# Decoder layer on one core: self and cross sums copied out in two halves, weighs in plain order, and maxima four further ahead

## The reference, cut to what matters

```python
q, k, v = _heads(x @ Wq + bq), _heads(x @ Wk + bk), _heads(x @ Wv + bv)       # 16 heads of 16
att = jnp.einsum('bhqd,bhkd->bhqk', q, k) * scale                            # causal, 512 x 512
y = jnp.einsum('bhqk,bhkd->bhqd', jax.nn.softmax(att, axis=-1), v)
qc, kc, vc = ...                                                              # from x and from the context
attc = jnp.einsum('bhqd,bhkd->bhqk', qc, kc) * scale                         # 512 x 1024
y = y + jnp.einsum('bhqk,bhkd->bhqd', jax.nn.softmax(attc, axis=-1), vc)
return y @ Wp + bp
```

## Time and profile before

| | |
|---|---|
| median of 3 runs | 2287.46 us (2287.35 to 2288.9) |
| the profiled execution | 2287.69 us |
| its span, first to last instruction | 2286.0 us |
| TensorE matmul busy | 2169.5 us (95%) |
| VectorE busy | 1366.7 us (60%) |
| ScalarE busy | 1102.2 us (48%) |
| GpSimdE busy | 367.5 us (16%) |

### The profile page before, as it was taken

One profiled execution on the slowest core, in us unless ns is written; L12 is line 12 of the kernel. 1 busy time (PEld: TensorE's weight loads), 2 busy tenths in 40 slices (PEclk: granted clock), 3 DMA queues, 4 the chain that ended last, 5 costly groups with the idle time before them and its releaser, 6 DMA issues. The chain is left out here.

```text
span 2286.0 us, 51067 instructions
## 1 busy us (share of the span) xinstructions
PE 2169.5 (95%) x16290; PEld 1352.2 (59%) x16291; DVE 1366.7 (60%) x3905; ACT 1102.2 (48%) x1680; POOL 367.5 (16%) x628
## 2 busy tenths in 40 slices
PE   8999999999899999999999999999999899799998
PEld 4555554556455555555555645554555455499997
DVE  2588357844785458635883478357844685255554
ACT  1267524761477227732674257524762377233332
POOL 1011111111111111111111111111111111122222
PEclk9999999999999999999999999999999999899999
DMA  7440025102520162005300350026102520655553
GB/s 235 155 164 25 2 106 200 48 2 85 198 71 2 47 234 73 2 11 189 130 25 9 141 180 25 1 97 209 48 2 85 198 71 2 221 181 182 183 182 109
DMA packets 115763, 235.75 MB, mean 103 GB/s; under 512 B 19614, under 2 KB 42655, under 8 KB 113344
## 3 DMA queue, kind: packets, MB, share of 16 engines
q1 hardware_dynamic: 112112, 224.23, 29.3%
q0 software_dynamic: 3408, 8.41, 1.0%
HBM read 154.04 MB, written 73.17 MB: 99 GB/s over the span
## 5 line engine op out<-in xcount | busy, mean ns | idle before, releaser
L1201 ACT ACTIVATE es<-ps 128x1024 f32<-128x1024 f32 (+1 forms) x704 | 665.3, 984 | 250.7 <-PE ps L809 181.4
L1412 DVE TENSOR_REDUCE craw<-ps 128x1 f32<-128x512 f32 x1024 | 636.7, 684 | 115.0 <-PE ps L773 115.0
L773 PE MATMUL ps<-hk,hq 64*128 64x512 f32 x1024 | 391.4, 450 | 24.7 <-DVE craw L1412 8.6
L807 PE MATMUL ps<-hq,hk 64*128 64x512 f32 x1024 | 325.0, 440 | 2.2 <-ACT es L1201 2.2
L1408 DVE CUSTOM_DVE_ANT_0 ps<-ps,causal 128x512 f32<-128x512 f32 (+3 forms) x512 | 236.2, 518 | 91.4 <-PE ps L770 91.0
L773 PEld LDWEIGHTS ps<-hk,hq 64*128 64x128 f32 x1024 | 174.7, 184 | 194.8 <-DVE craw L1412 129.3
L809 PE MATMUL ps<-mrow,minus 64*128 64x512 f32 x1024 | 285.8, 391 | 0.0
L837 PE MATMUL ps<-es,vca 128*17 128x256 f32 x4096 | 276.6, 382 | 1.2 <-ACT es L1201 0.3
L661 POOL TENSOR_SCALAR_AFFINE_SELECT es<-es 128x256 f32<-128x256 f32 x256 | 99.0, 406 | 659.5 <-ACT es L1201 659.4
L1731 ACT ACTIVATE hT<-ph,b1s 128x128 f32<-128x128 f32 x312 | 89.2, 369 | 182.8 <-PE ph L1694 182.8
L809 PEld LDWEIGHTS ps<-mrow,minus 64*128 64x128 f32 x1024 | 166.0, 186 | 10.1
(11 more groups left out here) (210 smaller groups left out, 2838.3 us busy)
## 6 DMA issues: line engine op xcount, KB each, us to landing
w1s<-in_w1T SPq DMA_DIRECT2D x39, 1024.0 KB, 5.4
hk<-scr_kc SPq DMA_DIRECT2D x64, 512.0 KB, 5.1
scr_kc<-staged SPq DMA_DIRECT2D x16, 1024.0 KB, 4.3
scr_qc<-staged SPq DMA_DIRECT2D x32, 512.0 KB, 4.5
scr_q<-staged SPq DMA_DIRECT2D x32, 512.0 KB, 5.3
hq<-scr_qc SPq DMA_DIRECT2D x56, 256.0 KB, 4.4
hq<-scr_q SPq DMA_DIRECT2D x56, 256.0 KB, 4.2
hk<-scr_k SPq DMA_DIRECT2D x56, 256.0 KB, 4.6
```

The lines of the kernel that those rows point to most:

```text
L773: last = mm(pb, hq[i][at, T + t * P:T + (t + 1) * P], hk[i][at, T + half * BANK:T + (half + 1) * BANK], start=True, stop=True)
L807: mm(pb[a], hk[i][rows[a], T + j * P:T + (j + 1) * P], hq[i][rows[a], T:2 * T], start=True, stop=False)
L1201: nc.scalar.activation(es[:, k % ERING, :].rearrange("p (a c) -> p a c", a=HB)[:, :, 0:w], eslot[k % 2][:].rearrange("p (a c) -> p a c", a ...
L1412: last = v.reduce_max(craw[p % 2][:, t, a:a + 1, 1 + half], pb, AX.X)
```

## The change

`keep` now has two parts. Part 0 copies the own half of `zbank` after the pair's third weigh (the last own one), part 1 the cross half after the eleventh. Each stands behind all weighs of its cycle, and waits on ScalarE until all weighs before it in the list are done (`KEEP_AFTER`). On TensorE a weigh waits for all copies that stand before it in the list, where it is a pair's first or where a copy stands between it and the weigh before (`KEPT_AT`). The turn waits for both.

No weigh is put off any more: the last weigh of a pair and the first of the next may stand together in a cycle, and the turn follows in the next cycle, ahead of the next pair's second weigh.

The first two cycles take two more maxima each (`MORE`, `MORE_CYCLES`), so that from then on all maxima stand one cycle earlier against scores and weighs. A row of maxima now stands only at the end of a cycle (or ahead of a projection's part), at the first such border that has at least four maxima behind the pair's last. Worked out from the list, it stands behind the same maxima as before, except the first, which now stands behind maxima 4 and 5 of pair 1, not ahead of them. The last row (pair 7) stands behind exp unit 5 of pair 6; before, it stood between units 6 and 7. Elsewhere a constant is only renamed.

```diff
--- before.py
+++ after.py
@@ -100,7 +100,9 @@
 MAXES = NMU * HB
 ERING = 4
 AHEAD = 8
-ROW_AFTER = (4, 6)
+ROW_AFTER = 4
+MORE, MORE_CYCLES = 2, 2
+CYCLE = 2
 BEHIND = 4
 LATER = 2
 
@@ -122,49 +124,42 @@
 def heads_order():
 
 
-    maxima = []
-    for p in range(PAIRS):
-        maxima += [("max", p, m) for m in range(MAXES)]
-    for p in range(PAIRS):
-        at = maxima.index(("max", p, MAXES - 1)) + 1 + (ROW_AFTER[p % 2] if p + 1 < PAIRS else 0)
-        maxima.insert(at, ("row", p, 0))
+    maxima = [("max", p, m) for p in range(PAIRS) for m in range(MAXES)]
+    order, rows, turns, kept = [], list(range(PAIRS)), [], []
 
     def take(count):
-        taken = []
-        while maxima and (count or maxima[0][0] == "row"):
-            count -= maxima[0][0] == "max"
-            taken.append(maxima.pop(0))
-        return taken
-
-    order = []
+        order.extend(maxima[:count])
+        del maxima[:count]
+
+    def row_if_due(behind):
+
+        p = rows[0] if rows else None
+        if rows and (PAIRS - p - 1) * MAXES - behind >= len(maxima):
+            order.append(("row", rows.pop(0), 0))
+
     for name, part, count in FIRST_PARTS:
-        order += take(count)
+        take(count)
+        row_if_due(ROW_AFTER)
         order.append(("part", name, part))
-    order += take(MAXES + AHEAD - sum(count for _, _, count in FIRST_PARTS))
-    turns, late = [], []
+    take(MAXES + AHEAD - sum(count for _, _, count in FIRST_PARTS))
     steps = PAIRS * NU
-    for k in range(0, steps + BEHIND, 2):
-        weighed = late + [m for m in (k - BEHIND, k - BEHIND + 1) if m >= 0]
-        late = []
+    for k in range(0, steps + BEHIND, CYCLE):
         if turns:
             order.append(turns.pop())
-        for m in weighed:
-            if m % NU == 0 and m and order[-1] == ("keep", m // NU - 1, 0):
-                late.append(m)
-                continue
+        for m in range(max(0, k - BEHIND), min(steps, k - BEHIND + CYCLE)):
             order.append(("weigh", *divmod(m, NU)))
-            if m % NU == NU - 1:
-                order.append(("keep", m // NU, 0))
+            if m % NU == NSELF - 1:
+                kept.append(("keep", m // NU, 0))
+            elif m % NU == NU - 1:
+                kept.append(("keep", m // NU, 1))
                 turns.append(("turn", m // NU, 0))
-        order += take(1)
-        if k < steps:
-            order.append(("exp", *divmod(k, NU)))
-        order += take(HB)
-        if k + 1 < steps:
-            order.append(("exp", *divmod(k + 1, NU)))
-        order += take(1)
-        order += [("weigh", *divmod(m, NU)) for m in late]
-        late = []
+        order.extend(kept)
+        kept = []
+        take(1)
+        for n in range(k, min(steps, k + CYCLE)):
+            order.append(("exp", *divmod(n, NU)))
+            take(HB if n + 1 < k + CYCLE else 1 + (MORE if k < MORE_CYCLES * CYCLE else 0))
+        row_if_due(min(ROW_AFTER, len(maxima)) if maxima else 0)
     assert not maxima
     return order + [("part", "qf2", 0)] + turns + [("part", "qf2", 1)]
 
@@ -192,11 +187,15 @@
 NEXP = PAIRS * NU
 
 
+KEPT_AT = {(p, n): sum(f[0] == "keep" for f in ORDER[:i]) for i, (kind, p, n) in enumerate(ORDER) if kind == "weigh"}
+KEEP_AFTER = {(p, n): sum(f[0] == "weigh" for f in ORDER[:i]) for i, (kind, p, n) in enumerate(ORDER) if kind == "keep"}
+
+
...
@@ -814,8 +813,8 @@
 
                 if p == 0 and n == 0:
                     pe.wait_ge(s_vone, b + 1)
-                if n == 0:
-                    pe.wait_ge(s_keep, cur(b, PAIRS, p))
+                if n == 0 or KEPT_AT[p, n] > KEPT_AT[p, n - 1]:
+                    pe.wait_ge(s_keep, cur(b, 2 * PAIRS, KEPT_AT[p, n]))
                 e, own = es[:, (p * NU + n) % ERING], n < NSELF
                 if own:
                     pe.wait_ge(s_cut, cur(b, PAIRS * NSELF, p * NSELF + n + 1))
@@ -841,7 +840,7 @@
             def turn_results(b, p):
 
                 pb = ring_slot(b, ("turn", p, 0))
-                pe.wait_ge(s_keep, cur(b, PAIRS, p + 1))
+                pe.wait_ge(s_keep, cur(b, 2 * PAIRS, 2 * p + 2))
                 for w in range(2):
                     for c in range(2):
                         col = (w * 2 + c) * P
@@ -1115,7 +1114,7 @@
         def _(act):
             act.sem_inc(s_mrow, PAIRS)
             act.sem_inc(s_exp, NEXP)
-            act.sem_inc(s_keep, PAIRS)
+            act.sem_inc(s_keep, 2 * PAIRS)
             act.sem_inc(s_zt, PAIRS - 1)
 
             def relu_q(i, t):
@@ -1202,12 +1201,12 @@
                                          eslot[k % 2][:].rearrange("p (a c) -> p a c", a=HB)[:, :, 0:w],
                                          ACT.Exp, scale=SCALE).then_inc(s_exp, 1)
 
-                def keep(p):
-
-                    act.wait_ge(s_av, cur(b, NEXP, (p + 1) * NU))
-                    if p:
+                def keep(p, w):
+
+                    act.wait_ge(s_av, cur(b, NEXP, KEEP_AFTER[p, w]))
+                    if p and w == 0:
                         act.wait_ge(s_ring, cur(b, NRING, RING_AT["turn", p - 1, 0] + 1))
-                    nc.scalar.activation(zk[:].rearrange("p w t -> p (w t)"), zbank, ACT.Copy).then_inc(s_keep, 1)
+                    nc.scalar.activation(zk[:, w, :], zbank[:, w * (T // 2):(w + 1) * (T // 2)], ACT.Copy).then_inc(s_keep, 1)
 
                 def turned(p):
 
@@ -1225,7 +1224,7 @@
                     elif kind == "exp":
                         exp_unit(p, n)
                     elif kind == "keep":
-                        keep(p)
+                        keep(p, n)
                     elif p == "v":
                         values()
                     elif p == "qc1":
...
```

More of the change, by code:

```diff
@@ L198 @@
 assert NTILE % 2 == 1
-MORE = T // TILE
+MORE_TILES = T // TILE
 CR = C + 1
@@ L343, in attentions @@
         upto = sb("upto", [P, NTILE])
-        full_at = sb("full_at", [P, MORE])
+        full_at = sb("full_at", [P, MORE_TILES])
         below = sb("below", [P, E + 1, E])
@@ L349, in attentions @@
         over = sb("over", [P, E])
-        more = sb("more", [P, E, MORE])
+        more = sb("more", [P, E, MORE_TILES])
         fresh = sb("fresh", [P, E])
@@ L1295, in _ @@
             v.tensor_scalar(upto[:, B * NT:NTILE], iota[:, 0:NTILE - B * NT], float(B * NT), None, ALU.add)
-            v.tensor_scalar(full_at[:], iota[:, 0:MORE], float(TILE), None, ALU.mult)
+            v.tensor_scalar(full_at[:], iota[:, 0:MORE_TILES], float(TILE), None, ALU.mult)
             v.tensor_tensor(below[:], iota[:, 0:E + 1].unsqueeze(2).broadcast_to([P, E + 1, E]),
@@ L1474, in _ @@
                 step(v.tensor_tensor(over[:], total, room[:], ALU.subtract))
-                step(v.tensor_tensor(more[:], over[:].unsqueeze(2).broadcast_to([P, E, MORE]),
-                                     full_at[:].unsqueeze(1).broadcast_to([P, E, MORE]), ALU.is_gt))
+                step(v.tensor_tensor(more[:], over[:].unsqueeze(2).broadcast_to([P, E, MORE_TILES]),
+                                     full_at[:].unsqueeze(1).broadcast_to([P, E, MORE_TILES]), ALU.is_gt))
                 step(v.reduce_sum(fresh[:], more[:], AX.X))
```

## The result

| | before | after |
|---|---|---|
| median | 2287.35 us (5 runs) | 2299.24 us (5 runs, 2298.66 to 2300.67) |
| ratio | | 1.0054, 95% interval 1.0039 to 1.0069 |
| profiled execution, its span | 2287.69, 2286.0 us | 2300.67, 2298.8 us |
| mean granted clock | 0.994 | 0.990 |

The changed kernel is 11.9 us slower, at the upper edge of the predicted range (2299) and just outside it.

The account below looks back on a forecast made before the run. TensorE, busy nearly all the time, was taken as the bound, VectorE close behind. Per batch -0.1 - 0.45 + 1.38 - 0.4 = +0.4 us, 3.1 in 8, gave 2290.5 us from 2287.46; range 2279 to 2299.

Parts of the forecast that it names:

- start, to M20 of pair 1: Head-loop start up to maximum 20 of pair 1: -0.45 us a batch (0 to -0.8).
- three periods, to M20 of the last pair: Repeating two-pair order, three times a batch: -0.04 us each, -0.1 a batch (bounds -1.5 and +1.2).
- tail: four cycles' E and W, ACT-paced: After the last pair's maximum 20: score and weigh cycles without maxima, paced by ScalarE, +1.38 us (0.9 to 1.9).
- tail: joined weighs, no stall on the exp: Later in the tail: two weighs stand together (-0.13 us) and a 0.27 stall goes; -0.4 us a batch.
- Half with the put-off weigh: Half-period that held the put-off weigh: 9.15 us becomes 9.39, +0.24, with a new 0.47 stall of the transposes.
- Other half: The period's other half: 12.60 us becomes 12.32, -0.28, though its transposes wait 0.23.
- M20-M1: Maxima 20 to 1 of the next pair, after turn and weighs: 2.05 us shrinks to 1.65 (1.58 to 2.05).
- rival B: Slower: M20-M1 doesn't shrink, its bank awaiting ScalarE's copy; +0.4 us a period, 2300 us, chance 0.2.
- Rival A: Clearly faster: the transposes' new waits (0.47 and 0.23 us) don't show; 0.70 a period, 2274 us, chance 0.2.
- Copies: Halved copies on ScalarE: 0.38 us each (0.30 to 0.60), hidden; uncovered they would cost 0.4 each, 26 in all.
- Start of the loop: First cycles: 14 maxima before the first weigh, VectorE the bound, weigh at about 1100.2 not 1097.81; -0.45 us.
- signs of being wrong: The period differing from 33.2 us by over 0.3, or a weigh waiting for a copy, would refute the forecast.

Follow-up runs that it names:

- e8: Kernel before with no weigh put off and the copy still whole, so the next pair's first weigh waits for it; 2318.98 us, ratio 1.0137.
- e4: Changed kernel plus nine filler matmuls of 256 columns behind maxima 11 to 19 of pair 1; 2332.48 us, ratio 1.0199.
- e1: Changed kernel without the four extra maxima in the first two cycles (no lead); 2278.17 us, ratio 0.9959.
- e2: Kernel before with only the lead added, two more maxima in each of its first two cycles; 2300.28 us, ratio 1.0056.
- e9: Changed kernel plus nine filler matmuls of 64 columns behind maxima 11 to 19 of pair 1; 2338.38 us, ratio 1.0226.
- e12: Changed kernel with half the lead, one more maximum instead of two in each of the first two cycles; 2298.34 us, ratio 1.0047.
- e6: Changed kernel without the lead and with each turn behind the two weighs of its cycle; 2265.27 us, ratio 0.9902.
- e5: Changed kernel, lead kept, with each turn behind the two weighs of its cycle instead of ahead; 2273.56 us, ratio 0.9954.

## Why the prediction was wrong

The forecast was +3.1 us, measured were +11.9. Taken in a batch whose clock stayed up (after, batch 5, against batch 4 of the earlier trace rows), the terms of the working hold but for the periods, of which more below:

| term, us a batch | predicted | measured |
|---|---|---|
| start, to M20 of pair 1 | -0.45 | -0.56 |
| three periods, to M20 of the last pair | -0.1 | +0.19 |
| tail: four cycles' E and W, ACT-paced | +1.38 | +1.39 |
| tail: joined weighs, no stall on the exp | -0.4 | -0.48 |
| sum | +0.4 | +0.54 |

(Batch 4 is among the longest before; against the mean the order costs 0.65.) In the profiled executions, whose spans differ by 12.8 us, the forecast so misses 9.7: 6.2 are the falls of the clock, 2.1 the order, 1.0 lies behind the last turn and 0.35 ahead of the first batch. Two slips in my sums change little: the last exp's end at 5.96 and 0.66 more are 6.62, not 6.67, and the four terms make 3.4 us in 8 batches, not 3.1.

*Half with the put-off weigh.* Right: 9.43 us (1391.21 to 1400.64) where 9.39 was said and 9.15 stood before. The turn's new stall is 0.47, as worked out.

*Other half.* Mis-sized. The stall of 0.23, the 1.79 of turn and weighs, and M20-M1 at 1.54 (1417.02 to 1418.56; 1.65 predicted, 2.05 before) came as said, so rival B is out. But the next piece with the row, M2-5, takes 2.44 us (1419.34 to 1421.78) and not 2.26: VectorE sets it, and what TensorE gains ahead of it is in part given back. 12.45 in sum from 1409.33 where 12.32 was forecast. Rival A is out too: both stalls show.

*Copies.* Right in size (0.385) and in that they are hidden; a weigh's weight loads wait 0.5 us once a batch, which I had not seen. e8 shows what a copy in the way costs: 0.97 us for a whole one of 0.60, so my 0.4 for an uncovered half one, its length alone, was likely too little; no run uncovers a half one.

*Start of the loop.* This is the step that failed. I wrote that 14 maxima come before the first weigh, "and DVE is the bound", and had the time of it right: the first weigh at 42.6 us in the batch, 42.85 predicted. I priced that stretch as waiting time alone, at the full clock that the earlier trace rows shows for a stretch where TensorE is busy. But there TensorE waits again and again: a maximum takes it 0.43 us (1118.06 to 1118.49 in e4's timeline) and VectorE 0.61 (ten in 6.07). With 2.2 us more of this its clock fell to 0.50 in half of the batches, which costs 0.7 to 2.4 us behind it where TensorE is the bound. That it is the lead which brings the falls is shown by e1 and e2 (with it they come, without it they go), and that it is what TensorE does in the stretch by e4 against e9; e12 has a fall behind another wait. Which batch falls stays open. It agrees with what the Trainium skill says on clock oscillation (TensorE: Matmul & The Clock Gate, HAM oscillation — how this bites in real kernels): a wait in the midst of a kernel can throttle TensorE again, and the work behind it starts slowly. Its example is a wait for DMA; here it is a chain of waits for VectorE, each of 1.0 us at most (the longest of its kind in a list of all waits), which is also the longest before, where the clock stayed up. The price of a fall is taken from the batches above. Neither of my signs of being wrong looked at the clock: the period kept within 0.3 us, and the weight loads that wait for a copy cost 3.7 us in all.

Outside the working lie 1.0 us behind the head loops, where a low stretch that all kernels have is longer in after and e2 (1988 to 2010 and 1986 to 2008 us, against 1976 to 1996); why, I haven't tested.

My working followed the order in time and never priced the change's two ideas apart. The traces do, in a batch without a fall (the fourth of each), cut at M20 of pair 1 and of the last pair:

| us | to M20 of pair 1 | three periods | to the last turn |
|---|---|---|---|
| before | 44.26 | 99.65 | 23.24 |
| e2, lead alone | 44.06 | 98.44 | 25.23 |
| e1, the rest alone | 43.99 | 99.73 | 22.09 |
| after, both | 43.74 | 99.94 | 24.12 |
| e6, e1 and the turn behind | 44.14 | 98.31 | 22.08 |
| e5, after and the turn behind | 43.75 | 97.28 | 24.12 |

The lead costs 2.0 us in the tail in each of the three pairs (my +1.38 was against the old place of the row, so it stood in the forecast as the largest term, hidden behind what the rest gains). It wins 1.2 us in the periods of the kernel before and 1.0 with the turn behind the weighs, but nothing in the changed kernel, where the turns wait 17.9 us in all, 8.6 without the lead. That is most of why the lead costs 13 us on the kernel before and 21 on e1. And the halved copies with no weigh put off leave the periods as they were (99.73); what e1 gains lies in the tail, over half of it by the place of the last row as its trace reads, and at the start.

## What to carry to other kernels

Where TensorE is the bound nearly everywhere, look at the few stretches where it isn't: lengthening one can drop its clock, and the price is paid later, at half speed, in the stretch where it is the bound again. Price such a term with both clocks, and read the mean granted clock beside each execution's time; where the times of one kernel scatter, it tells whether the clock goes with them. And when a change has two parts, work out each alone: here the version with one of them and a turn moved behind two weighs (e6) is 1.0% faster than the kernel before and 1.5% faster than the changed one. Then look at how they meet: here one part took away what the other would have won.

## What the runs showed of the hardware

- A filler of 128 rows and 64 columns in fp32, recorded as two matmuls, took 0.37 us to the next maximum (e9), one of 256 columns 0.63 (e4): a quarter of the columns is far from a quarter of the time, so "free" work for TensorE in its idle time isn't free.
- One kernel's executions differed by 21.5 us, and of what was recorded of each only the mean granted clock (0.995 to 0.984) goes with it.
- From PSUM, ScalarE's copy of 128x256 fp32 took 385 ns and of 128x512 603, so halving an instruction cost 167 ns more in all.
